# Attention decoder kernel: ScalarE's order in the narrow cross attention, the feed-forward maxima and up pass over three engines, and a late loop placed at a multiple of 256 slots

## The reference, cut to what matters

```python
def _act_fake_quant(x, clip_factor):
    scale = jax.nn.sigmoid(clip_factor) * jnp.max(jnp.abs(x)) / QMAX   # one scale for the whole tensor
    return jnp.clip(_ste_round(x / scale), -QMAX - 1.0, QMAX) * scale
# h      = _act_fake_quant(layernorm(x), clip_x)
# hidden = silu(h @ w_gate.T) * (h @ w_up.T)                           # 352 hidden features
# y      = _act_fake_quant(hidden, clip_down) @ w_down.T
```

## Time and profile before

| | us |
|---|---|
| Median of 3 runs | 2507.98 (2504.81 to 2511.05) |
| Profiled execution, its own time | 2510.14 |
| Span in the trace | 2508.3 |
| PE busy | 2190.0 (87%) |
| VectorE busy | 1960.5 (78%) |
| ScalarE busy | 1448.3 (58%) |
| GpSimd busy | 1216.1 (48%) |

### The profile page before, as it was taken

How to read it: one execution, slowest core, us unless ns; L and a number is a source line. 1 busy time by engine, 2 the same in 40 slices (tenths; PEclk the granted TensorE clock), 3 DMA queues, 4 the chain that set the end, 5 groups by cost and what they waited for, 6 DMA issues and landing times. The chain is left out here.

```text
span 2508.3 us, 90125 instructions
## 1 busy us (share of the span) xinstructions
PE 2190.0 (87%) x33097; PEld 1802.9 (72%) x33103; DVE 1960.5 (78%) x5517; ACT 1448.3 (58%) x3893; POOL 1216.1 (48%) x1198
## 2 busy tenths in 40 slices
PE   7999999977777752237999989999999999999998
PEld 7888888865555541136888768887788888888886
DVE  3888888868999978897888667775777777777775
ACT  1666666646666642346888768886444444444443
POOL 0333333327777752008999789996222323222232
PEclk9999999989999986758999989999999999999999
DMA  4000000000000000000000000000000000000000
GB/s 120 3 0 0 0 0 0 0 7 21 17 17 17 17 8 0 0 25 11 0 0 0 1 2 0 0 0 4 8 12 14 10 13 10 10 13 10 13 10 14
DMA packets 56941, 25.64 MB, mean 10 GB/s; under 512 B 18115, under 2 KB 56326, under 8 KB 56838
## 3 DMA queue, kind: packets, MB, share of 16 engines
q1 hardware_dynamic: 53426, 23.06, 3.4%
q10 hardware_dynamic: 3412, 1.19, 0.2%
HBM read 20.04 MB, written 4.19 MB: 10 GB/s over the span
## 5 line engine op out<-in xcount | busy, mean ns | idle before, releaser
L704 POOL TENSOR_TENSOR sa_sc<-sa_sc,sa_rs 128x1024 f32<-128x1024 f32 x64 | 121.9, 1904 | 316.0 <-DVE sa_rs L680 316.0
L1820 POOL TENSOR_TENSOR lo_qk_r<-lo_qk_ms,w_neg_half 128x20 f32<-128x20 f32 x64 | 226.9, 3545 | 22.0 <-DVE lo_qk_ms L1743 21.9
L1820 POOL TENSOR_TENSOR gl_qk_r<-gl_qk_ms,w_neg_half 128x20 f32<-128x20 f32 x64 | 226.6, 3541 | 1.4 <-DVE gl_qk_ms L1743 1.4
L484 POOL TENSOR_TENSOR xan_ve<-xan_mv,w_eps_ln 128x1 f32<-128x1 f32 x64 | 12.1, 189 | 399.6 <-DVE xan_mv L478 399.6
L890 ACT ACTIVATE xa_cT<-xa_misc 128x128 f32<-128x128 f32 x64 | 17.8, 278 | 303.8 <-PE xa_misc L791 274.0
L1014 POOL TENSOR_TENSOR xa_sc<-xa_sc,xa_rs 128x1024 f32<-128x1024 f32 x64 | 121.7, 1901 | 118.5 <-DVE xa_rs L974 118.5
L819 PEld LDWEIGHTS xa_qs<-xan_xT,late_x_wq 128*128 128x128 f32 x1024 | 119.3, 192 | 52.8 <-issue 52.8
L556 PE MATMUL sa_qs<-san_xT,w_a_wq 128*128 128x128 f32 x1024 | 132.0, 283 | 2.6 <-DVE sa_sc L666 2.2
L971 DVE TENSOR_REDUCE xa_sm<-xa_sc 128x16 f32<-128x1024 f32 x64 | 78.1, 1220 | 69.7 <-ACT xa_sc L914 69.7
L819 PE MATMUL xa_qs<-xan_xT,late_x_wq 128*128 128x128 f32 x1024 | 131.4, 282 | 0.0
L830 PE MATMUL xa_pp<-xa_cT,late_x_wk 128*128 128x128 f32 x1024 | 131.1, 281 | 0.0
(11 more groups left out here) (328 smaller groups left out, 6859.6 us busy)
## 6 DMA issues: line engine op xcount, KB each, us to landing
w_x<-in_x_dram SPq DMA_DIRECT2D x8, 512.0 KB, 7.6
ca_cx<-in_ctx_dram SPq DMA_DIRECT2D x64, 64.0 KB, 1.8
xa_cx<-in_ctx_dram SPq DMA_DIRECT2D x64, 64.0 KB, 1.8
out_dram<-xa_out SPq DMA_DIRECT2D x64, 64.0 KB, 1.6
ca_mask<-in_mask_BxSxS_ff_dram SPq DMA_DIRECT2D x64, 32.0 KB, 1.7
w_a_wq<-in_L_attn_Wq_dram SPq DMA_DIRECT2D x1, 512.0 KB
w_a_wo<-in_L_attn_Wout_dram SPq DMA_DIRECT2D x1, 512.0 KB
prep_xwo<-in_L_xattn_Wo_dram ACTq DMA_DIRECT2D x1, 512.0 KB
```

Source lines behind the costliest of these rows:

```text
L704: pool.tensor_tensor(v, v, bcast(rs[:, s, :], 2, S), ALU.mult).then_inc(prob_done, 1)
L1820: pool.tensor_tensor(qk_r[:, s, :], qk_ms[:, s, :], k["neg_half"][:, 0:NQK], ALU.pow).then_inc(sg["qk_r"], 1)
```

## The change

It has four parts.

```diff
-def skewed(eng, n, pieces, unroll=2):
+def skewed(eng, n, pieces, unroll=2, whole_blocks=False):
...
     if start < n:
+        if whole_blocks:
+            eng.addr_align(256, max_nops=0)
         with eng.Fori(start // unroll, n // unroll) as i:
...
-                                (1, keys), (3, output), (8, turn_back)], 4)
+                                (1, keys), (3, output), (8, turn_back)], 4, whole_blocks=True)
...
-                skewed(act, NT, [(2, queries_keys), (2, values), (1, turned), (4, exponent), (5, probsT)], 4)
+                skewed(act, NT, [(2, queries_keys), (1, turned), (2, values), (4, exponent), (5, probsT)], 4)
...
+                def apply(g, s):
+                    after(act, offset_done, g)
+                    for n in range(GROUP):
+                        act.activation(tile_of(H, g * GROUP + n), tile_of(X, g * GROUP + n), ACT.Identity,
+                                       bias=offset[:, s, n:n + 1], scale=rstd[:, s, n:n + 1]).then_inc(normed, 1)
+
+                skewed(act, NG, [(2, apply)], 4)
...
+                def offsets(g, s):
                     after(dve, rstd_done, g)
+                    after(dve, normed, g, 4, per=GROUP)
+                    dve.scalar_tensor_tensor(out=offset[:, s, :], in0=mv[:, s, :, 0], scalar=-1.0, in1=rstd[:, s, :],
+                                             op0=ALU.mult, op1=ALU.mult).then_inc(offset_done, 1)
+
+                def largest(g, s):
+                    after(dve, normed, g, per=GROUP)
+                    cols = slice(g * GW, (g + 1) * GW) if isinstance(g, int) else bass.ds(g * GW, GW)
+                    to = xmax[:, g:g + 1] if isinstance(g, int) else xmax[:, bass.ds(g, 1)]
+                    dve.tensor_reduce(to, H[:, cols], AX.X, ALU.max, apply_absolute_value=True).then_inc(top_done, 1)
+
+                skewed(dve, NG, [(2, offsets), (0, statistics), (4, largest), (0, mean_variance)], 4)
+                dve.wait_ge(top_done, NG)
+                dve.tensor_reduce(top[:, 0:1], xmax[:, :], AX.X, ALU.max).then_inc(top_done, 1)
-                skewed(dve, NG, [(2, apply), (0, statistics), (0, mean_variance)])
-                dve.wait_ge(normed, NT)
-                dve.tensor_reduce(top[:, 0:1], H[:, :], AX.X, ALU.max, apply_absolute_value=True).then_inc(top_done, 1)
...
-                skewed(pool, NG, [(0, rsqrt)])
-                pool.wait_ge(top_done, 1)
+                pool.memset(amax[:, :, :], 0.0)
+                skewed(pool, NG, [(0, rsqrt)], 4)
+                pool.wait_ge(top_done, NG + 1)
...
-            xr = sb2("xr", [P, 2, GW])
-            xq = sb2("xq", [P, 2, GW], BF16)
+            xr = sb2("xr", [P, 4, GW])
+            xq = sb2("xq", [P, 4, GW], BF16)
...
-                    skewed(dve, NG, [(3, hidden(0)), (0, clip_high), (3, hidden(1)), (0, clip_low), (3, hidden(2)), (0, integers)])
-                    dve.wait_ge(h_done, 3 * NG)
-                    for c, (f0, fn) in enumerate(FCH):
-                        last = dve.tensor_reduce(amax[0:fn, c:c + 1], HT[0:fn, c, :], AX.X, ALU.max, apply_absolute_value=True)
+                    def largest(g, s):
...
+                        after(dve, h_done, g, per=3)
+                        dve.tensor_reduce(amax[:, at, 0:2].rearrange("p g c -> p (g c)"), HT[:, 0:2, cols], AX.X, ALU.max, apply_absolute_value=True)
+                        dve.tensor_reduce(amax[0:96, at, 2], HT[0:96, 2, cols], AX.X, ALU.max, apply_absolute_value=True).then_inc(top2, 1)
+
+                    skewed(dve, NG, [(5, hidden(0)), (2, integers), (5, hidden(1)), (5, hidden(2)), (6, largest)], 4)
...
+                    def clipped(g, s):
+                        after(pool, r1, g)
+                        gate(k, pool)
+                        pool.tensor_scalar(xr[:, s, :], xr[:, s, :], MAGIC + QMAX, MAGIC - QMAX - 1.0, ALU.min, ALU.max).then_inc(r2, 1)
+
+                    skewed(pool, NG, [(1, clipped)], 4)
...
-                    skewed(pe, NG, [(1, turn), (2, products)])
+                    skewed(pe, NG, [(3, turn), (4, products)], 4)
...
+                    def scaled(g, s):
+                        after(act, q_done, g, 4)
+                        act.activation(xr[:, s, :], group_of(H, g), ACT.Copy, bias=MAGIC, scale=sinv[:, 0:1]).then_inc(r1, 1)
...
-                    skewed(act, NG, [(1, turned), (2, silu)])
+                    skewed(act, NG, [(3, turned), (0, scaled), (4, silu)], 4)
```

More of the change, by code:

```diff
@@ L1260, in ffn @@
         identb = sb("identb", [P, P], BF16)
-        amax = sb("amax", [P, 3])
+        amax = sb("amax", [P, NG, 3])
+        xmax = sb("xmax", [P, NG])
+        offset = sb("offset", [P, 4, GROUP])
         top = sb("top", [P, 2])
@@ L1285, in scale_steps @@
             dve.reciprocal(sinv[:, n:n + 1], sact[:, n:n + 1]).then_inc(scales[n], 1)
-        e_done, top_done, all_done, cleared = sem("exp_clip"), sem("top"), sem("all_top"), sem("cleared")
+        e_done, top_done, all_done, offset_done = sem("exp_clip"), sem("top"), sem("all_top"), sem("offset")
         with nc.Block() as block:
@@ L1306, in mean_variance @@
                         dve.bn_aggr(mv[:, s, n, :], stats[:, s, n, :]).then_inc(mv_done, 1)
-                def apply(g, s):
+                def offsets(g, s):
                     after(dve, rstd_done, g)
[L1310 to L1315, removed]
-                skewed(dve, NG, [(2, apply), (0, statistics), (0, mean_variance)])
-                dve.wait_ge(normed, NT)
-                dve.tensor_reduce(top[:, 0:1], H[:, :], AX.X, ALU.max, apply_absolute_value=True).then_inc(top_done, 1)
+                    after(dve, normed, g, 4, per=GROUP)
+                    dve.scalar_tensor_tensor(out=offset[:, s, :], in0=mv[:, s, :, 0], scalar=-1.0, in1=rstd[:, s, :],
[8 more added lines that the diff above has]
+                dve.tensor_reduce(top[:, 0:1], xmax[:, :], AX.X, ALU.max).then_inc(top_done, 1)
                 dve.wait_ge(e_done, 1)
@@ L1346, in ffn @@
             up = [ps2(f"u{n}") for n in range(3)]
-            r1, r2, q_done, t_psum, t_done = sem2("clip_high"), sem2("rounded"), sem2("quantised"), sem2("xT_psum"), sem2("xT")
+            r1, r2, q_done, t_psum, t_done = sem2("rounded"), sem2("clipped"), sem2("quantised"), sem2("xT_psum"), sem2("xT")
             g_psum, u_psum, s_done, h_done = sem2("gate_psum"), sem2("up_psum"), sem2("silu"), sem2("hidden")
@@ L1356, in _ @@
                 def _(dve):
-                    def clip_high(g, s):
-                        dve.tensor_scalar(xr[:, s, :], group_of(H, g), sinv[:, 0:1], QMAX, ALU.mult, ALU.min).then_inc(r1, 1)
-                    def clip_low(g, s):
-                        after(dve, r1, g)
-                        dve.tensor_scalar(xr[:, s, :], xr[:, s, :], -QMAX - 1.0, MAGIC, ALU.max, ALU.add).then_inc(r2, 1)
                     def integers(g, s):
                         after(dve, r2, g)
-                        after(dve, t_psum, g, 2)
+                        after(dve, t_psum, g, 4)
                         dve.tensor_scalar(xq[:, s, :], xr[:, s, :], MAGIC, None, ALU.subtract).then_inc(q_done, 1)
@@ L1379, in hidden @@
                         return piece
[L1381 to L1387 removed]
+                    def largest(g, s):
+                        cols = slice(g * GW, (g + 1) * GW) if isinstance(g, int) else bass.ds(g * GW, GW)
+                        at = slice(g, g + 1) if isinstance(g, int) else bass.ds(g, 1)
+                        after(dve, h_done, g, per=3)
+                        dve.tensor_reduce(amax[:, at, 0:2].rearrange("p g c -> p (g c)"), HT[:, 0:2, cols], AX.X, ALU.max, apply_absolute_value=True)
+                        dve.tensor_reduce(amax[0:96, at, 2], HT[0:96, 2, cols], AX.X, ALU.max, apply_absolute_value=True).then_inc(top2, 1)
+                    skewed(dve, NG, [(5, hidden(0)), (2, integers), (5, hidden(1)), (5, hidden(2)), (6, largest)], 4)
+                    dve.wait_ge(top2, NG)
+                    dve.tensor_reduce(top[:, 1:2], amax[:, :, :].rearrange("p g c -> p (g c)"), AX.X, ALU.max).then_inc(top2, 1)
                     scale_steps(dve, 1, all2)
@@ L1402, in turn @@
                         for n in range(GROUP):
-                            last = pe.transpose(tp[s][:, n * P:(n + 1) * P], xq[:, s, n * P:(n + 1) * P], identb[:, :])
+                            last = pe.transpose(tp[s % 2][:, n * P:(n + 1) * P], xq[:, s, n * P:(n + 1) * P], identb[:, :])
                         last.then_inc(t_psum, 1)
```

18 lines of the change are left out of this document (7 added, 11 removed).

## The result

The changed kernel takes 2473.8 us (median of 3 runs, 2471.66 to 2474.45) against 2507.98: a ratio of 0.9862, interval 0.9839 to 0.9884. The profiled execution took 2471.66 us, 38.5 less than that of before.

A forecast was written before the change was run, and what follows sets the result against it. VectorE bounds the narrow cross, one serial path feed-forward, PE the late loop. Gains 15.7 (feed-forward) + 3.6 (narrow cross) + 0 = 19.3 us against 2510.14: 2490.8, or 2489 on the median's scale; 8 in 10 from 2478 to 2500.

The forecast's parts named there:

- What bounds each place: Narrow cross: VectorE, 92% busy; up pass before: no engine full; late loop: PE, busy 559.99 of 560 us.
- feed-forward is one serial path: Feed-forward, norm to last long reductions: all that is shortened there shortens the kernel, as the down pass needs the maximum.
- B: Norm's apply on ScalarE, first maximum in the loop: 38.1 to 32.5 us; everything gained is spent on the reconfigurations.
- A: Narrow cross, ScalarE's transposed-input copy ahead of values: 0.056 us a tile, 3.6 us gained, bounds 0 and 4.5.
- but then `ca_oT` is the last, 0.07 us earlier: Narrow cross: with `ca_xcT` earlier, the output product still waits for `ca_oT`; a tile gains at most 0.07 us.
- L: Time of one GpSimd reconfiguration, ahead of the first all-reduce and first clip: 7.5 us taken, between nothing and 9.2.
- the second one: New GpSimd reconfiguration ahead of the up pass's first clip: holds that clip up by 7.5 us, to 975.7.
- the third one: GpSimd reconfiguration ahead of the second all-reduce: hidden, as the last clip is over 16 us before the last maximum.
- The estimate by the 6 us: Reconfigurations at about 6 us each, by the Trainium skill: 3 us more of gain, 2486.
- C: Up pass over three engines: 4.13 us a group, VectorE bounds; last maximum at 1049.4 against 1065.08, 15.7 us gained.
- D: Late loop's new place: 0 gained, at most 0.01 us, as the loop is not fetched anew in a pass.
- The first one: Rival: reconfigurations are cheap, under 2.5 us; at 0 another 12.4 us gained, 2476; chance 0.10.

The follow-up runs named there:

- e5: The changed kernel with ScalarE's value copies in two halves around the copy of the transposed input: ratio 0.9856, 2475.1 us.
- e11: The changed kernel with VectorE's `can_xn` moved ahead of the reciprocal and ScalarE's old order (values ahead of the transposed input): ratio 0.9898, 2483.7 us.
- e9: The changed kernel with the norm's aggregates right behind the statistics again, the group's maximum behind them: ratio 0.9863, 2475.5 us.
- e13: The changed kernel with the late weights' load held back until GpSimd has made global attention's first reciprocal deviation: ratio 0.9848, 2470.1 us.
- e4: The kernel before with the late loop's new place alone: ratio 0.9996, 2508.9 us.
- e7: The changed kernel with both all-reduces of GpSimd replaced by a PE multiplication with the identity and a VectorE maximum: ratio 0.9806, 2461.3 us.
- e14: The changed kernel with the up pass of before: ratio 0.9898, 2481.9 us.

## Why the prediction was wrong

**What bounds each place, and that feed-forward is one serial path: right.** What went from it was gained. The forecast had all that B gains spent on the reconfigurations ahead of the first `hidden`; in the traces 7.9 us of it are left there (11.3 + 4.4 - 7.8).

**A: wrong in its reason, and 3.6 for 11.9 us (10 on average over the traces).** The step that failed is "but then `ca_oT` is the last, 0.07 us earlier". I took it from a wait of PE's that the trace puts down to `ca_oT`. The code says otherwise: `output` has lag 7 and `normalise` lag 6, so the product needs the `ca_oT` of the step before, ready a tile earlier, and in the changed kernel's timeline it starts ahead of the one that it was said to wait for. With that limit gone, the apply bounds the residual; and there I held its recorded end for the earliest start, where VectorE starts a next instruction that waits for nothing 0.08 us ahead of it. e5 (threshold) and e11 (the copy is what the product waits for) show the first, the timeline the second. The 52 tiles of the loop by 0.16 are 8 us; the rest lies in the steps written out ahead of and behind it, 2.2 us of it between the last `can_mv` and the feed-forward block. That last stretch scatters: 31.1 to 32.6 us in the kernels with the old order, 30.3 to 31.7 with the new one.

**B: mechanism right, sizes off.** Norm: 32.5 forecast, 26.8 measured. The sum has a slip that hid part of the miss: it takes off 16 applies of 1.01 us, but those of the last two groups stand behind the last aggregate, at 962.88 to 965.59 us. With 14 it is 34.6, so the other terms were 7.8 us too long. Of the 0.53 us that a group with maxima was put too long (2.40 - 1.01 + 0.20 + 0.65 = 2.24 against 1.71), 0.26 is the aggregates' wait for the statistics, which e9 shows to be covered by the maximum between them; 0.15 is the offset, which costs its spacing, 0.05, and not its duration; 0.07 the maximum, 0.58; 0.05 stays open. At 12 such groups that is 6.4 us. The rest is the loop's turns, which the sum left as they were: before, a turn made every second group 0.43 us longer (2.83 instead of 2.40), and the changed list, with four groups in its body, has two longer groups (1.94 and 2.04).

**The reconfigurations: found, and right in what they do; L was 7.5, and it measured 5.7 and 6.9.** The all-reduce waits for L and not for the maximum, which gives the first maximum its 1.8 us; the second one holds up the first clip, and the third one is hidden: right. The first clip comes 7.8 us behind the block's start (944.75 us on ScalarE, where GpSimd's reconfiguration starts at 945.71), so 7.5 was near there. L came from the one row that had transfers beside it, and e13 shows that those are worth 3 us. The estimate by the 6 us of the Trainium skill ("GPSIMD Engine Reference", 2.1 Instruction dispatch) was nearer for the all-reduce.

**C: right.** From the up block's start to the first `hidden` 14.25 us forecast, 14.0 measured (14.5 from `ff_sup`, half a microsecond ahead of the block); 4.13 us a group forecast (its terms add to 4.12), 4.03 measured; VectorE bounds, silu's wait is gone, and no `integers` is held up by a clip. The clip costs 0.61 us where I had 1.0 to 1.9, which moves nothing but the fill.

**D: right**, nothing (e4).

**The rivals.** None came. The first one had the sign, and its 2476 us lies near the 2474 measured by luck: L was not small. The range was too narrow below, since I put bounds on L alone and none on the norm's group, and held A's upper bound (4.5 us) for hard while it hung on one reading.

## What to carry to other kernels

Before a tile is said to wait for something, work out from the lags which tile's work the waiting instruction reads: the profile names what came last in time, which may be a tile too young. Price a VectorE instruction by the distance to the next start in a row without waits, and look for a semaphore wait on the engine's own last result: an independent instruction put between is nearly free. Here each change to GpSimd's all-reduce and back took 5.4 to 7.6 us, more beside transfers, and it cost time wherever no other wait covered it; read the engine's order for them. Keep GpSimd's wide instructions from starting just ahead of VectorE's apply.

## What the runs showed of the hardware

- A reconfiguration of GpSimd ahead of an all-reduce takes 5.4 to 6.0 us where nothing else covers it, the first one behind an all-reduce 6.7 to 7.6 us where DMA engines are idle, and 9.2 to 10.7 us beside the late weights' loads (204 GB/s in the changed kernel, 211 before; e13: 7.1 without them, same place). With no all-reduce between, the row stands in the queue and the next instruction starts 0.1 us (e7's first clip) to 0.7 us behind it.
- GpSimd's clip of 128 x 512 (minimum and maximum with constants) takes 0.61 us, less than the 0.95 that half of its 1.90 us subtraction gives, and 0.85 us where VectorE's `integers` starts 0.04 us ahead of it.
- VectorE's apply of 128 x 128 takes 0.34 us if it starts 0.17 us ahead of GpSimd's wide subtraction, which then takes 1.93 us instead of 1.90. It takes 0.82 to 0.95 us if it starts 1.04 to 1.16 us behind the subtraction's start, and ends 0.08 us behind its end.
- The same wide self-attention took 500.3 to 500.8 us in the seven traces where the clock granted from 45 to 80 us was 0.90 to 0.95 of full speed, and 503.6 to 505.4 us in the nine where it was 0.76 to 0.85. One kernel does both, it seems: the nine runs of the kernel before beside e13 and e14 took 2504.9 to 2505.7 us (five, mean clock 0.951) or 2510.1 to 2512.2 us (four, 0.947 to 0.950). What sets the clock there stays open.
